# Moving two small phases of a graph network kernel under the phases beside them: the marking of first edges and the first linear map

## What is computed

```
s = s @ W_nl0                                    # first linear map (layer 0), per node
v = einsum('nmi,mk->nki', v, W_nl1)
w = relu(edge_feature @ W_fc1) @ W_fc2           # 224 weights per edge
xs, xv = s[dst], v[dst]                          # gathered per edge
tp = concatenate([w0*xs, w3*dot(xv, sh1), ...])  # messages
agg = segment_sum(tp, src) / 32                  # summed by src
...
den = segment_sum(ex, dst)                       # layer 1: attention, summed by dst
```

## Time and profile before

| | us |
|---|---|
| median of 3 runs | 27698.21 |
| lowest and highest | 27689.18, 27711.11 |
| the profiled execution, its own time | 27672.57 |
| its span | 27670.8 |

### The profile page before, as it was taken

One profiled execution on the slowest core, in us unless ns is written; L12 is line 12 of the kernel. 1 busy time (PEld: TensorE's weight loads), 2 busy tenths in 40 slices (PEclk: granted clock), 3 DMA queues, 4 the chain that ended last, 5 costly groups with the idle time before them and its releaser, 6 DMA issues. The chain is left out here.

```text
span 27670.8 us, 473394 instructions
## 1 busy us (share of the span) xinstructions
PE 20086.8 (73%) x102170; PEld 15592.6 (56%) x102170; DVE 19967.8 (72%) x70146; ACT 11898.4 (43%) x39928; POOL 12223.8 (44%) x11987
## 2 busy tenths in 40 slices
PE   0046656666478888888888888883677788677788
PEld 0023322222367777777777777772555677555677
DVE  5911158888378888888888888886777666777666
ACT  0022234444356666666666666663333222333222
POOL 0277746666134444444444444440777300777300
PEclk9677778888788888888888888885999888999998
DMA  4033345555322222222222222222222200222200
GB/s 146 28 110 121 121 95 112 111 111 110 88 76 73 73 73 73 73 73 73 73 73 73 73 73 73 73 73 62 65 61 61 32 5 5 65 60 60 33 5 5
DMA packets 1703933, 1962.55 MB, mean 71 GB/s; under 512 B 745521, under 2 KB 1345025, under 8 KB 1703233
## 3 DMA queue, kind: packets, MB, share of 16 engines
q0 software_dynamic: 565056, 1310.16, 18.0%
q1 hardware_dynamic: 1138816, 651.71, 9.2%
HBM read 1399.54 MB, written 561.06 MB: 71 GB/s over the span
## 5 line engine op out<-in xcount | busy, mean ns | idle before, releaser
L1485 PE MATMUL e_sums<-e_feat,e_same 128*128 128x272 f32 x13824 | 3444.8, 403 | 1357.1 <-ACT e_feat L1506 1231.1
L1467 POOL DMA_INDIRECT e_rows<-x,e_take x3456 | 3620.8, 1048 | 1120.4 <-issue 1048.5
L1017 POOL DMA_INDIRECT e_srow<-src_table,e_take x1620 | 1557.5, 961 | 5323.3 <-issue 5172.7
L1485 PEld LDWEIGHTS e_sums<-e_feat,e_same 128*128 128x128 f32 x13824 | 2595.1, 192 | 2206.5 <-issue 1596.0
L549 PE MATMUL e_sums<-e_feat,e_same 128*128 128x480 f32 x3456 | 1956.7, 722 | 1301.5 <-DVE e_feat L617 1301.3
L1052 PE MATMUL e_ps_m<-ident,e_m 128*128 128x128 f32 x12960 | 2332.8, 308 | 575.1 <-DVE e_m L1248 415.7
L533 POOL DMA_INDIRECT e_rows<-table,e_take x1728 | 1935.6, 1120 | 1302.1 <-issue 1273.9
L1052 PEld LDWEIGHTS e_ps_m<-ident,e_m 128*128 128x128 f32 x12960 | 1592.1, 159 | 1260.2 <-DVE e_m L1248 769.3
L1066 PEld LDWEIGHTS e_ps_x<-ident,e_lg 128*128 128x128 f32 x12960 | 2169.6, 237 | 76.2
L549 PEld LDWEIGHTS e_sums<-e_feat,e_same 128*128 128x128 f32 x3456 | 799.6, 244 | 2458.2 <-issue 2383.3
L1066 PE MATMUL e_ps_x<-ident,e_lg 128*128 128x128 f32 x12960 | 2125.1, 319 | 0.0
(11 more groups left out here) (306 smaller groups left out, 52361.5 us busy)
## 6 DMA issues: line engine op xcount, KB each, us to landing
e_pay<-pay_rows SPq DMA_DIRECT2D x432, 470.0 KB, 3.7
firsts_keys<-key_row SPq DMA_DIRECT2D x270, 384.0 KB, 3.5
e_keys<-key_row SPq DMA_DIRECT2D x1620, 64.0 KB, 2.8
e_rows<-x,e_take POOLq DMA_INDIRECT x3456, 2.6
order_feat<-in_attr_T SPq DMA_DIRECT2D x810, 64.0 KB
comb<-n_comb SPq DMA_DIRECT2D x300, 164.0 KB, 1.9
e_rows<-table,e_take POOLq DMA_INDIRECT x1728, 4.0
pay_rows<-order_stage,order_put POOLq DMA_INDIRECT x1620, 2.5
```

What stands on the lines that cost most here:

```text
L1017: pool.indirect_dma_start(out=srow[t.j][:, :], out_offset=None, in_=src_table, in_offset=bass.IndirectOffsetOnAxis(ap=takes[0][t.j][:, :], ...
L1467: pool.indirect_dma_start(out=rows[t.j][:, q, :], out_offset=None, in_=x, in_offset=bass.IndirectOffsetOnAxis(ap=take[t.j][:, q:q + 1], ax ...
L1485: ins = pe.matmul(sums[b][q // G][:, 512 * h:512 * h + HALF], same[b][:, q, :], feat[b][:, q, h * HALF:(h + 1) * HALF], start=q % G == 0, ...
```

## The change

The phase `firsts` is gone. Its comparisons are made in the sending loop of `order`, two per pair, on VectorE after its two copies; the keys are loaded per pair (128 KB) into three buffers, on SyncE ahead of the pair's features. Its last four operations stand after the loop. The phase `n0` is gone too. Its work on SyncE, TensorE and ScalarE stands at the start of the same engines' blocks of `order`, and the copy out of PSUM is ScalarE's now. TensorE waits for all 50 tiles of it before it sums the counts, and SyncE waits for its stores before the loop's loads.

```
+        earlier, work = scan, part[0]
+        keys = [ph.sb(f"keys{k}", [P, 2 * P]) for k in range(RING // 2)]
+        hit = [ph.sb(f"hit{k}", [P, 2 * P]) for k in range(2)]
...
             @block.sync
...
+                load_matrix(sp, WN, A["w0_nl"], nl)
+
+                def node(s):
+                    if s.exists():
+                        if s.reuses(2):
+                            sp.wait_ge(turned, s.count(-1))
+                        sp.dma_start(row[s.j][:, 0:D], x[bass.ds(s.t() * P, P), :]).then_inc(row_in[s.j], 16)
+                    b = s.back(1)
+                    if b.exists():
+                        sp.wait_ge(map_set, b.count(1))
+                        sp.dma_start(table[bass.ds(b.t() * P, P), :], mapped[b.j][:, :]).then_inc(stored[b.j], 16)
+                run_steps(sp, node, 1, 2, NB)
+                for k in range(2):
+                    sp.wait_ge(stored[k], 16 * (NB // 2))
 
                 def step(t):
+                    q = t.j % 3
+                    if t.reuses(3):
+                        sp.wait_ge(hits, t.count(-2))
+                    sp.dma_start(keys[q][:, :], g.key_row[bass.ds(t.t() * (2 * P), 2 * P)].partition_broadcast(P)).then_inc(keys_in[q], 16)
                     if t.reuses(RING):
                         sp.wait_ge(hid_ps, t.count(1 - RING))
                     sp.dma_start(feat[t.j][:, :], A["attr64_T"][:, bass.ds(t.t() * P, P)]).then_inc(feat_in[t.j], 16)
...
             @block.tensor
...
+                node_steps(pe, node)
+                pe.wait_ge(map_set, NB)
                 pe.wait_ge(counted, 1)
...
             @block.scalar
+                def node(b):
+                    act.wait_ge(turned, b.count(1))
+                    if b.reuses(2):
+                        act.wait_ge(map_ps, b.count(-1))
+                    act.activation(rowT[b.j][:, :], ps_h[b.j][:, 0:2 * P], ACT.Copy).then_inc(turned_sb, 1)
+                    act.wait_ge(map_ps, b.count(1))
+                    if b.reuses(2):
+                        act.wait_ge(stored[b.j], b.dma(1))
+                    act.activation(mapped[b.j][:, :], ps_w[b.j][:, 0:D], ACT.Copy).then_inc(map_set, 1)
+                node_steps(act, node)
...
             @block.vector
...
                     dve.tensor_copy(stage[t.j][:, :, WNUM:PAY], own[:, bass.ds(t.t() * 2, 2), :]).then_inc(own_set, 1)
+                    dve.wait_ge(keys_in[t.j % 3], t.value(32, 32 * t.off + 16 * (t.j // 3 + 1)))
+                    if t.reuses(2):
+                        dve.wait_ge(hits, t.count(-1))
+                    for q in range(2):
+                        n = t.t() * 2 + q
+                        ins = dve.scalar_tensor_tensor(
+                            out=hit[t.j % 2][:, q * P:(q + 1) * P], in0=keys[t.j % 3][:, q * P:(q + 1) * P],
+                            scalar=g.key_f[:, bass.ds(n, 1)], in1=g.before[:, :],
+                            op0=ALU.is_equal, op1=ALU.mult, accum_out=earlier[:, bass.ds(n, 1)])
+                    ins.then_inc(hits, 1)
                 run_steps(dve, step, 0, RING, PAIRS)
...
             with ExitStack() as sorting:
                 own = allocate(sorting)("own", [P, NT, OWN])
                 prepare(nc, g, A, own)
-                first_edges(nc, g)
-                order_edges(nc, g, A, own, pay_rows)
-            first_table(nc, g, A, A["x"], table0)
+                order_edges(nc, g, A, own, pay_rows, A["x"], table0)
```

137 lines of the change are left out of this document (31 added, 106 removed).

## The result

| | before | with the change |
|---|---|---|
| median of 4 runs on the same chip, us | 27703.97 | 26836.44 |
| lowest and highest | 27689.18, 27711.11 | 26817.98, 26863.15 |
| the profiled execution, its own time | 27672.57 | 26817.98 |
| its span | 27670.8 | 26815.9 |

The ratio is 0.9689, with a 95% interval of 0.9677 to 0.9701: 867.5 us faster by the medians, 854.9 us by the spans of the two profiled executions. I had forecast 26,863 us, with 26,790 to 26,990 as the range.

A forecast was written before the change was run, and what follows sets the result against it. No single engine bounds the kernel: each phase between barriers costs its slowest engine, GpSimd's transfers in the sending loop. -768.9 - 159.0 + 53 + 40 = -835 us, giving 26,863 us by the median; range 26,790 to 26,990.

The forecast's parts named there:

- The two phases out: Marking of first edges and first linear map no longer stand as phases: -768.9 us and -159.0 us.
- The map into the counting phase: VectorE waits for TensorE's sum of the counts behind the map, mostly at slow clock: +53 us, ends 30 and 57.
- first rival: Map hides better: TensorE keeps 2.4 GHz and no mark collides, wait 30 us; 26,800 us, chance 0.13.
- The marks on VectorE: Sending loop: two marks add 0.6 to 0.9 us a pair to VectorE, against 2.53 us; hidden, no cost.
- The marks against GpSimd's issue: Sending loop: transfers starting while a mark runs are held to its end; +40 us, with landings 0.2 us late.
- second rival: Sending loop: landings move 0.4 us or more, so marks cost +134 instead of +40; 26,957 us, chance 0.15.
- my own overlay: Mark offsets laid over 316 pairs of the loop: 10 us lost as landings stand, 43 at 0.2 later, 134 at 0.4 to 0.6.
- The full lock: Sending loop: marks start only when a transfer ends, 259 us instead of 40; 27,082 us, chance 0.08.
- The tail: Four whole-width operations after VectorE's last pair, at most 7.4 us, begin 12.6 us before GpSimd ends; nothing.
- The key loads: Sending loop: 128 KB of keys a pair on SyncE cost no time; DMA share about +0.16 on 0.38.
- The key slots: Sending loop: VectorE's step hangs on key loads, slower than before at 10.5 us landings; 27,957 us, chance 0.02.
- The later phases: Phases downstream of the sending loop, from the edge layer on: untouched, no change in time.

The follow-up runs named there:

- the long key packets: Changed kernel with keys loaded for three pairs at once (3 KB a partition instead of 1 KB) into two buffers, fourth chip: 26,856.7 us.
- the marks without loads: Changed kernel with the marks made on three key tiles that are loaded only once, second chip: sending loop 2427.1 us.
- the triangle in PSUM: Changed kernel with the triangle of ones copied once to PSUM, so a mark reads one SBUF tile, third chip: 28,040.5 us.
- the marks alone: Changed kernel with the first map a phase of its own again, only the marking moved, second chip: 28,148.4 us, ratio 0.9757.

## Why the prediction was right

- **The two phases out** (-768.9, -159.0): read off the borders, and exact to 0.1 us. A phase that stands alone between two barriers is worth its whole length.
- **The map into the counting phase** (+53): measured +52.0. The wait was put where it came, at VectorE's copy of the total, because I looked at what was queued behind the map on TensorE; moving the sum ahead of it took the wait away whole. My working had the map's first load, its length alone and its turn of 6.03 us as in its own phase; it was 5.98 (144.60 to 150.58). That TensorE would not speed up was right, and so the first rival's 26 us fell. The sign by which I meant to see it was wrong: the granted clock reads 1.00 there (below).
- **The marks on VectorE** ("hidden"): shown. GpSimd never waited longer than 0.3 us for a copy. Of the 12 us of slack some were used: a pair's copies ended at least 9.9 us before its transfer before, and at least 7.7 us with the change.
- **The marks against GpSimd's issue** (+40): the mechanism was right and the term too large by 27 us, or by 29 without the 2.3 us of the last operations. The mechanism, a transfer held to the end of an operation with two inputs from SBUF, was read from one pair of rows of the edge layer, and the 109 held transfers follow it (each ends 0.83 to 0.84 us after its mark). Two inputs of the working failed, in opposite directions. First, I took landings 0.2 us late. From the start of a pair's second transfer to the copy that waits for the pair's slot it is 2.66 us in the median before and 4.45 with the change: 1.8 us late. (Against the latest transfer's start the copies stand at 0.65 us where they had stood at 0.13, but such an offset hides a whole period of 1.265.) So the condition of my second rival came true, and by my own overlay it would have cost 134 us. Second, I let a mark hold any transfer that starts within its 0.35 us; only starts 0.09 to 0.22 us after it are held, by 0.13 us at most. With holds so short the lateness decides little: where the copies start only 0.3 us later than before (the long key packets, 2.93 us) or 0.1 (the marks without loads, 2.81), 103 and 74 transfers are still over 1.0 us. The kind of the term was foreseen; that its size came as near as it did was luck, since the two errors cancelled in part.
- **The full lock** (third rival, 259 us): did not happen. The Trainium skill ("SBUF — State Buffer", SBUF: two separate sides and Who interferes with whom) says that an instruction of VectorE with two inputs from SBUF contends with a GpSimd instruction that reads SBUF, and that whichever starts first has the ports for the whole instruction while the other is blocked. Where VectorE comes first, the runs bear it out: the held transfers go on when the mark has ended, and the triangle in PSUM took them from 90 to 2. Where an indirect transfer comes first, they do not: 1141 marks started inside a transfer, and none of them took over 0.36 us. The rival needs just that. What a transfer takes of the ports is short: it lengthened only marks that had started at most 0.09 us before it, by 0.07 us at most. For GpSimd's addition they bear out both, with the scan's 6.80 us against 3.59.
- **The tail** ("nothing"): 2.3 us of held transfers by the four whole-width operations, and 1.5 us more at the phase's end. I had asked only whether VectorE was done in time, not what these operations do to GpSimd. For most of the work in the loop I had asked both.
- **The key loads** ("nothing"): right in time on the first chip, wrong in the DMA share (0.63 for 0.55), because I scaled by bytes from loads with rows of 3 KB, and these have 1 KB. On the chips with stalls they cost 40 us.
- **The key slots** (fourth rival, 0.02): my sign for it was that VectorE waits for keys. On the chip of the result VectorE waited 2.6 us for keys. On the third chip it waited 920 us, and the loop lost 59.5 us, not the 1100 that the rival needs. A chance of 0.02 for a slower kernel was no mistake, but my only number for a landing came from one chip.
- The later phases differ by 6.2 us; four kernels with the same later phases had 23,937 to 23,955 us in them on the fourth chip, a spread of 18. I read nothing into it.

## What to carry to other kernels

A phase between two barriers that uses engines idle elsewhere is worth its whole length, and the price of moving it is found by asking what stands behind it in each queue: put what another engine is waiting for ahead of it, and the price can be next to nothing (52 us and 0.3 us here). Before laying one engine's work beside another's, look at an operation's shortest record against its median; a factor like 3.59 to 6.80 us within one line can mean that the two already hold each other (here it did), and moving a small operation to the engine that it blocks can be worth more than sharing the work. When traffic is estimated from another load, scale by packets as well as by bytes.

## What the runs showed of the hardware that I had not expected

- VectorE's scan over 1620 columns takes 3.59 us alone and 6.80 us if GpSimd's addition of two SBUF tiles (3.98 us) began 0.56 us before it. An indirect transfer beside it does not lengthen it; the transfer takes 3.88 us instead.
- A transfer that starts in such an operation ends some 0.8 us after the operation does: 338.83 against 338.06 for the scan, 340.78 against 339.95 for the product, 342.66 against 341.82 for the addition, and 0.83 to 0.84 us after a mark of 0.35 us. It seems held some 0.13 us after its start and then does the rest.
- The granted clock of a stretch does not always tell TensorE's speed. The map has the same products in two kernels; in its own phase, in the kernel with the marks alone, the row reads

```profile
3270.00:3440.00 170.00, 99.45 (x300) 68.76 (x300) 16.49 (x52) 19.20 (x50) 0.91 (x2) 0.50 0.20 56
```

and in the change 1.00 with a busy time of 100.58 us (x304). The products' records are alike, 1.43 us. In the change this is TensorE's first work in the program, and no change of the clock is recorded before 226.9 us; until one is, a row reads 1.00, as it does for the marking phase of the kernel before, in which TensorE did nothing. The Trainium skill ("TensorE: Matmul & The Clock Gate", Seeing it yourself) warns that the clock's events in a profile have been seen to be unreliable. Here it is not a wrong event but the lack of one that misleads; the durations decide.
- Of four chips two ran the same kernel before 4.1 and 4.2% slower than the first. In the sending loop this shows as stops of GpSimd, 130 of them over 0.35 us in the kernel before on the third chip. In long stretches it is 4 us every 24 us (before 1667.6, 1691.6 and 1715.5 us), which is every eight pairs and not the loop's turn of six. GpSimd waits for ScalarE's copy in most of them (109 times, 325 us), behind idle times of TensorE for which the profile names no releaser. No run of mine tells their cause.
